# Counting edges by 16 destinations and 8 groups of sources instead of 32 and 4, with the diagonal, the degrees, the folded biases and the loop registers handled otherwise

## The reference

```python
xn = _layernorm(x)
x = x + gnn(xn, edges, L0_gnn_W, L0_gnn_b) + mix(xn, Wq, bq, Wk, bk, Wv, bv, Wo, bo, P)
x = x + ffn(_layernorm(x), Wg, Wu, Wd, Wr, temperature)
# gnn: edges (row, col) = (src, dst), and a self edge (n, n) for every node
h = xn @ W.T + b
deg = zeros(N).at[row].add(1.0)
norm = deg[row] ** -0.5 * deg[col] ** -0.5
out = segment_sum(norm[:, None] * h[col], row, N)
# mix: linear attention, 16 heads of 64; features relu(P . q) and relu(P . k)
# ffn: 8 experts of 128 hidden units, gated silu, routing weights
```

## Time and profile before

| | |
|---|---|
| three runs | 1119.9, 1120.11, 1120.98 us |
| the profiled execution | 1121.14 us, of which the span from first to last instruction is 1119.2 us |
| PE (matmuls) busy | 1098.6 us, 98% of the span, 5707 instructions |
| DVE, ACT, POOL busy | 369.6, 252.9, 287.5 us |
| mean granted TensorE clock | 0.997 |
| counting matmuls | 178 in the fixed parts, 40 in the loops, 40 for self edges |

### The profile page before, as it was taken

One profiled execution on the slowest core, in us unless ns is written; L12 is line 12 of the kernel. 1 busy time (PEld: TensorE's weight loads), 2 busy tenths in 40 slices (PEclk: granted clock), 3 DMA queues, 4 the chain that ended last, 5 costly groups with the idle time before them and its releaser, 6 DMA issues.

```text
span 1119.2 us, 15481 instructions
## 1 busy us (share of the span) xinstructions
PE 1098.6 (98%) x5707; PEld 911.8 (81%) x5707; DVE 369.6 (33%) x991; ACT 252.9 (23%) x398; POOL 287.5 (26%) x232
## 2 busy tenths in 40 slices
PE   5999999999999999999999999999999999999998
PEld 4888778877878888888878888887888888888887
DVE  6854665665623111222212113344321111111111
ACT  4330211112223244311111112334121111112000
POOL 5000011121222146510034443434132223325000
PEclk9999999999999999999999999999999999999999
DMA  6303011222223497704079987775022222216321
GB/s 242 114 29 104 13 29 54 62 61 64 67 91 105 153 306 243 246 1 151 28 193 325 308 242 209 223 225 146 1 86 61 61 61 61 71 52 216 105 102 66
DMA packets 144518, 139.29 MB, mean 124 GB/s; under 512 B 6636, under 2 KB 114492, under 8 KB 144189
## 3 DMA queue, kind: packets, MB, share of 16 engines
q1 hardware_dynamic: 143868, 136.20, 39.0%
q10 hardware_dynamic: 576, 2.10, 0.5%
HBM read 102.32 MB, written 35.96 MB: 124 GB/s over the span
## 4 chain that ended last, share of the span: by engine, by line
PE 97%; DVE 1%; ACT 1%; DMA 1%; issue 0%; POOL 0%; DVEq 0%
PE ps L1549 10%; PE ps L1551 10%; PE ps L1550 10%; PE ps L1817 7%; PE ps L1819 6%; PE ps L1818 6%; PE ps L1759 4%; PE ps L1753 4%; PE ps L1676 3%; PE ps L1677 3%; PE ps L1678 3%; PE ps L1733 3%; PE ps L1865 3%; PE ps L1735 3%; PE ps L1734 3%; PE ps L1864 3%
## 5 line engine op out<-in xcount | busy, mean ns | idle before, releaser
L1549 PE MATMUL ps<-w_hi,xnH 128*128 128x512 f32 x480 | 191.4, 399 | 0.2 <-POOL w_lo L686 0.2
L1550 PE MATMUL ps<-w_lo,xnH 128*128 128x512 f32 x480 | 187.3, 390 | 0.0
L1551 PE MATMUL ps<-w_hi,xnL 128*128 128x512 f32 x480 | 187.2, 390 | 0.0
L1549 PEld LDWEIGHTS ps<-w_hi,xnH 128*128 128x128 f32 x480 | 90.3, 188 | 19.8 <-POOL w_lo L686 0.7
L1551 PEld LDWEIGHTS ps<-w_hi,xnL 128*128 128x128 f32 x480 | 90.2, 188 | 19.4
L1550 PEld LDWEIGHTS ps<-w_lo,xnH 128*128 128x128 f32 x480 | 90.3, 188 | 17.6
L732 POOL TENSOR_TENSOR acc<-acc,cw 128x320 f32<-128x320 f32 x40 | 35.3, 883 | 260.9 <-ACT cw L904 260.0
L1676 PE MATMUL ps<-xnH,w_hi 128*128 128x512 f32 (+1 forms) x192 | 69.2, 360 | 0.0
L1677 PE MATMUL ps<-xnL,w_hi 128*128 128x512 f32 (+1 forms) x192 | 68.3, 356 | 0.0
L1678 PE MATMUL ps<-xnH,w_lo 128*128 128x512 f32 (+1 forms) x192 | 68.0, 354 | 0.0
L1817 PE MATMUL ps<-x2H,guH 128*128 128x512 f32 (+1 forms) x192 | 67.6, 352 | 0.4 <-ACT wT L1084 0.4
(11 more groups left out here) (313 smaller groups left out, 2058.2 us busy)
## 6 DMA issues: line engine op xcount, KB each, us to landing
cR<-c_d SPq DMA_DIRECT2D x20, 640.0 KB, 5.2
foldin<-in SPq DMA_DIRECT2D x32, 256.0 KB, 2.8
guR<-in SPq DMA_DIRECT2D x16, 512.0 KB, 5.3
c_d<-cw SPq DMA_DIRECT2D x40, 160.0 KB
w_raw<-in SPq DMA_DIRECT2D x12, 512.0 KB, 6.5
xb<-in SPq DMA_DIRECT2D x10, 512.0 KB, 4.8
qs0H<-qT_d SPq DMA_DIRECT2D x10, 512.0 KB, 5.4
qs0L<-qT_d SPq DMA_DIRECT2D x10, 512.0 KB, 6.5
```

Source lines behind the costliest of these rows:

```text
L1549: pe.matmul(target, xnH[:, kc, cols], wH[w][:, kc, :], start=(kc == 0), stop=False)
L1550: pe.matmul(target, xnH[:, kc, cols], wL[w][:, kc, :], start=False, stop=False)
L1551: mm = pe.matmul(target, xnL[:, kc, cols], wH[w][:, kc, :], start=False, stop=(kc == KC - 1))
```

## The change

- The first 384 destinations are counted in 24 windows of 16, the others in 28 pairs of windows (32 destinations); sources in 8 groups of 160. A narrow window's matmul has 160 columns and 128 rows (8 groups x 16 destinations). For a pair, `hot1` has 256 places and PE runs two 160-column matmuls per chunk on the same `hot2`. Two narrow windows or one pair share a PSUM bank and are copied, stored and added together, so these are 40 as before.
- `SHARE` sums to 147 instead of 178. With the inputs' sorted destinations, counted out, the loops run 28 times in the 24 narrow windows and 35 times in the 28 pairs. The last fixed chunk of a window stands behind the loop and closes it.
- Self edges: no matmul; POOL adds the identity to each block of C when it is loaded (`own_edges`), and ACT's `count_high` waits for that (`c_own`). The degrees get + 1 from DVE.
- Degrees: two matmuls of 160 columns into 8 x 160, to memory and back as 128 x 10; DVE and ACT use them at j = 5, 6 and 8 instead of 1, 3 and 4.
- Folded biases: one 2-column matmul for both, of each of eight blocks; the result is 128 x 8 and goes to memory in 4-byte pieces.
- Registers: one load of four (two narrow windows) or two (a pair), when a PSUM bank is opened, behind the wait for `win_out`.
- POOL no longer makes `id16`, `idq` and `shifted`; DVE has four more instructions in `edges_keys`.

```diff
-WIN = 32
-NWIN = NP // WIN
-SRCG = NP // 4
-NCHX = NCH + WIN
-SHIFT = SRCG - WIN
+
+WIN = 16
+GROUPS = P // WIN
+SRCG = NP // GROUPS
+NPAIR = NP // (2 * WIN)
+NARROW = 24
+NWIN = NARROW + NPAIR - NARROW // 2
+NCHX = NCH + 32
 RING = 12
-SHARE = [25, 11, 8, 7, 6, 6, 5, 5, 5, 5] + [4] * 7 + [3] * 22 + [1]
+SHARE = [17, 7, 6, 4, 4, 3, 4, 3, 3, 3, 3] + [2] * 13 + [3] * 8 + [2] * 20
...
+def _pair(w):
+
+    return (w // 2, (w % 2,)) if w < NARROW else (w - NARROW // 2, (0, 1))
...
+PAIR_SEEN = [0] + [SEEN[w + 1] for w in range(NWIN) if 1 in _pair(w)[1]]
...
 
-            def store_window(w):
-                t, k = w // 4, w % 4 * WIN
-                sp.wait_ge(win_out, w + 1)
-                sp.dma_start(c_d[t][k:k + WIN, :].rearrange("j (g c) -> g j c", g=4), cw[:, w % 3, :])\
-                  .then_inc(c_st[w % 3], 16)
+            def store_pair(q):
+                t, k = q // 4, q % 4 * 2 * WIN
+                sp.wait_ge(win_out, q + 1)
+                for h in range(2):
+                    rows = c_d[t][k + h * WIN:k + (h + 1) * WIN, :].rearrange("j (g c) -> g j c", g=GROUPS)
+                    sp.dma_start(rows, cw[:, q % 3, h * SRCG:(h + 1) * SRCG]).then_inc(c_st[q % 3], 16)
...
-            sp.dma_start(fb_d[:, :], fbrow[:]).then_inc(fb_st, 16)
+            sp.wait_ge(bias_ev, 2)
+            with nc.allow_non_contiguous_dma(reason="1024 sums"):
+                sp.dma_start(fb_d.rearrange("o (c q) -> q (o c)", q=P), bkf[:]).then_inc(fb_st, 16)
...
+                if j == 2:
+                    sp.wait_ge(dg, 1)
+                    sp.dma_start(deg_d.rearrange("(g c) -> g c", g=GROUPS), drow[:]).then_inc(deg_st, 16)
+                if j == 3:
+                    sp.wait_ge(deg_st, 16)
+                    with nc.allow_non_contiguous_dma(reason="1280 degrees"):
+                        sp.dma_start(dtmp[:, 0, :], deg_d.rearrange("(t q) -> q t", q=P)).then_inc(in_deg, 16)
...
+            def own_edges(i):
+                t, k = i % NT, i // NT * 2 + i % 2
+                pool.wait_ge(in_c[i % 2], 16 * (i // 2 + 1))
+                pool.tensor_tensor(cR[k][:, t, :], cR[k][:, t, :], ident[:], ALU.add).then_inc(c_own, 1)
...
-            def window_out(w):
-                act.wait_ge(win_mm, w + 1)
-                if w >= 3:
-                    act.wait_ge(c_st[w % 3], 16 * (w // 3))
-                    act.wait_ge(acc_step, w - 2)
-                act.activation(cw[:, w % 3, :], bank(6 + w % 2, SRCG), ACT.Copy).then_inc(win_out, 1)
+            def pair_out(q):
+                act.wait_ge(hot_used, PAIR_SEEN[q + 1])
+                if q >= 3:
+                    act.wait_ge(c_st[q % 3], 32 * (q // 3))
+                    act.wait_ge(acc_step, q - 2)
+                act.activation(cw[:, q % 3, :], bank(6 + q % 2, 2 * SRCG), ACT.Copy).then_inc(win_out, 1)
...
-            def hot_pair(target1, target2, w, column, ready):
-                dve.tensor_scalar(target1, iota[:, 0:P], key1[:, column], -512.0 * w, ALU.subtract, ALU.is_equal)
-                dve.tensor_scalar(target2, iota[:], key2[:, column], None, ALU.is_equal).then_inc(ready, 1)
+            def hot_pair(hot_rows, hot_cols, w, column, ready):
+                q, halves = _pair(w)
+                n = len(halves) * P
+                dve.tensor_scalar(hot_rows[:, 0:n], iota[:, 0:n], key1[:, column], -float(2 * P * q + P * halves[0]),
+                                  ALU.subtract, ALU.is_equal)
+                dve.tensor_scalar(hot_cols, iota[:, 0:SRCG], key2[:, column], None, ALU.is_equal).then_inc(ready, 1)
...
-                if end == SEEN[w + 1]:
-                    stop = dve.value_load(rng[0:1, 1, w:w + 1], min_val=2, max_val=NCHX - 1)
-                for n in range(begin, end):
+                closes = end == SEEN[w + 1]
+                if begin == SEEN[w] and 0 in _pair(w)[1]:
+                    k = 2 if w < NARROW else 1
+                    dve.load(span[0:2 * k], rng[0:1, w:w + k, :].rearrange("o w k -> o (w k)"))
+                    for i in range(k):
+                        ranges[w + i] = (dve.snap(span[2 * i], min_val=0, max_val=NCH - 1),
+                                         dve.snap(span[2 * i + 1], min_val=2, max_val=NCHX - 1))
+                first, stop = ranges[w]
+
+                def counted(n):
                     if n >= RING:
                         dve.wait_ge(hot_used, n - RING + 1)
                     hot_pair(hot1[:, n % RING, :], hot2[:, n % RING, :], w, bass.ds(first + (n - SEEN[w]), 1), hot_ready)
-                if end < SEEN[w + 1]:
+
+                for n in range(begin, end - 1 if closes else end):
+                    counted(n)
+                if not closes:
                     return
                 p = w % 2
                 with dve.Fori(first + SHARE[w], stop) as j:
...
+                counted(end - 1)
...
                 if j == 1:
                     dve.wait_ge(deg_mm, 1)
-                    dve.tensor_copy(dtmp[:, 0, :], bank(6, NT)).then_inc(dg, 1)
-                    dve.tensor_reduce(degi[:, 0:1], bank(6, NT), AX_X, ALU.max).then_inc(dg_max, 1)
-                if j == 4:
+                    dve.tensor_scalar(drow[:], bank(6)[0:GROUPS, 0:SRCG], 1.0, None, ALU.add).then_inc(dg, 1)
+                if j == 5:
+                    dve.wait_ge(in_deg, 16)
+                    dve.tensor_reduce(degi[:, 0:1], dtmp[:, 0, :], AX_X, ALU.max).then_inc(dg_max, 1)
+                if j == 8:
...
             def folded_biases():
                 pe.wait_ge(in_const, 48)
                 for c in range(KC):
-                    pe.matmul(bank(6 + c // 4)[0:1, c % 4 * P:(c % 4 + 1) * P], bkc[:, c:c + 1], pbd_s[:, c, :],
-                              start=True, stop=True)
-                for c in range(KC):
-                    mm = pe.matmul(bank(5)[:, c:c + 1], pbd_s[:, c, :], bqc[:, c:c + 1], start=True, stop=True)
+                    mm = pe.matmul(bank(5)[:, 2 * c:2 * c + 2], pbd_s[:, c, :], bkq[:, :, c], start=True, stop=True)
...
             def window(w, begin, end):
-                p, target = w % 2, bank(6 + w % 2, SRCG)
-                if w >= 2:
-                    pe.wait_ge(win_out, w - 1)
-                else:
-                    pe.wait_ge(edge_step, EDGE_STEPS)
-                    pe.wait_ge(consts, CONSTS)
-                for n in range(begin, end):
+                p, (q, halves) = w % 2, _pair(w)
+                if 0 in halves and begin == SEEN[w]:
+                    if q >= 2:
+                        pe.wait_ge(win_out, q - 1)
+                    else:
+                        pe.wait_ge(edge_step, EDGE_STEPS)
+                        pe.wait_ge(consts, CONSTS)
+                    k = 2 if w < NARROW else 1
+                    pe.load(span[0:2 * k], rng[0:1, w:w + k, :].rearrange("o w k -> o (w k)"))
+                    for i in range(k):
+                        ranges[w + i] = (pe.snap(span[2 * i], min_val=0, max_val=NCH - 1),
+                                         pe.snap(span[2 * i + 1], min_val=2, max_val=NCHX - 1))
+                first, stop = ranges[w]
+                closes = end == SEEN[w + 1]
+
+                def count(hot_rows, hot_cols, used, opening=False, closing=False):
+                    for i, h in enumerate(halves):
+                        mm = pe.matmul(bank(6 + q % 2)[:, h * SRCG:(h + 1) * SRCG], hot_rows[:, i * P:(i + 1) * P], hot_cols,
+                                       start=opening and h == 0, stop=closing and h == 1)
+                    mm.then_inc(used, 1)
+
+                for n in range(begin, end - 1 if closes else end):
                     pe.wait_ge(hot_ready, n + 1)
-                    pe.matmul(target, hot1[:, n % RING, :], hot2[:, n % RING, :], start=(n == SEEN[w]), stop=False)\
-                      .then_inc(hot_used, 1)
-                if end < SEEN[w + 1]:
+                    count(hot1[:, n % RING, :], hot2[:, n % RING, :], hot_used, opening=n == SEEN[w])
+                if not closes:
                     return
-                first = pe.value_load(rng[0:1, 0, w:w + 1], min_val=0, max_val=NCH - 1)
-                stop = pe.value_load(rng[0:1, 1, w:w + 1], min_val=2, max_val=NCHX - 1)
                 with pe.Fori(first + SHARE[w], stop):
                     n = pe.snap(rests[p])
                     pe.wait_ge(rest_ready[p], n + 1)
-                    pe.matmul(target, rest1[:, p, :], rest2[:, p, :], start=False, stop=False)\
-                      .then_inc(rest_used[p], 1)
+                    count(rest1[:, p, :], rest2[:, p, :], rest_used[p])
                     pe.reg_add(rests[p], rests[p], 1)
-                g, col = w // 10, SHIFT + w // 10 * WIN - w % 10 * WIN
-                pe.matmul(target, idq[:, g, :], shifted[:, col:col + SRCG], start=False, stop=True)\
-                  .then_inc(win_mm, 1)
+                pe.wait_ge(hot_ready, end)
+                count(hot1[:, (end - 1) % RING, :], hot2[:, (end - 1) % RING, :], hot_used, closing=True)
...
```

(59 more changed lines are left out.)

135 lines of the change are left out of this document (66 added, 69 removed).

## The result

| | before | after |
|---|---|---|
| median | 1120.55 us (1119.9 to 1121.38) | 1144.58 us (1142.89 to 1147.16, 4 runs) |
| span of the profiled execution | 1119.2 us | 1145.4 us |
| mean granted clock | 0.997 | 0.988 |
| all counting portions, each up to the next other matmul | 39.4 us for 258 matmuls | 53.4 us for 309 |

The runs of before are those made beside after, with the first three. The ratio is 1.0219 (95% interval 1.0202 to 1.0236): the change makes the kernel slower by 24 us. The forecast was 1104.5 us, with 0.94 on faster. It was wrong in sign. The profiled execution of after is the slowest of its four, so that the two traces part by 26 us and the medians by 24.

A forecast was written before the change was run, and what follows sets the result against it. PE, busy 98% of the span, was taken to bound the kernel. Terms -13.5 + 4.5 - 1.8 - 1.75 - 3.1 = -15.65 took 1121.1 to 1105.5, and the median 1.0 lower to 1104.5 us; 8 in 10 range 1100 to 1112.

The forecast's parts named there:

- counting matmuls and stalls: PE's counting steps: 309 matmuls at 0.069 us instead of 258 at 0.135, -13.5 us; stalls of PE's queue, +4.5 us.
- folded biases: Stage 0: 16 two-column matmuls instead of 32 instructions, -1.8 us; the result's 4-byte pieces cost 0.
- degrees, and the clock's old falls: Four 160-column instructions for the degrees, -1.75 us; both old falls to about half clock gone, -3.1 us.
- identity in C: POOL's add between C's load and ACT's copy, under 0.5 us; PE comes 1.7 us later, so 0.
- DVE behind it: Counting steps: DVE, busy 130 of 218 us, makes 210 one-hot pairs instead of 218 and has more room: 0.
- the store: Folded-bias result in 1024 4-byte pieces, bounded by a 5.2 us load of 1280 pieces, wanted some 60 us later: 0.
- The third rival: PE waits for SP's small pieces (degree store, 4-byte load, fold inputs in one queue): 1126.5 us, slower than before; chance 0.03.
- the counting matmul: A 160-column f16 counting matmul on PE costs 0.069 us, if the next weights load beside it within 0.067 us.
- the rival of weight loads: Weight loads set the counting matmuls' pace, 0.112 us per 160 columns: 1115.3 us; chance 0.10.
- a third opening: Counting steps closing two banks and opening a third, where PE can't queue: six of 1.3 us, 8 us.
- The rival on the clock: Six stretches with over 1 us of stall in the counting steps call the clock down: 1112.4 us; chance 0.12.

The follow-up runs named there:

- experiment 6: The kernel after with one fixed chunk more in the 11 twice-looping windows and the folded-bias store and reload behind the folds' inputs: 1105.34 us, ratio 0.9874 against before.
- experiment 1: The kernel after with SHARE raised by one in the 11 windows whose loop runs twice, so every loop runs once: 1112.33 us, ratio 0.9939 against before.
- experiment 4: The kernel after with the store and load of the folded bias moved behind the last fold input of stage 0 in SP's queue: 1137.76 us.
- experiment 2: The kernel before with SHARE lowered by one in 11 windows, whose loops then run twice: 1157.64 us, ratio 1.0331 against before.
- experiment 3: The kernel after with second passes kept, but two buffers per parity for the loops' one-hots, used in turn: 1119.99 us, ratio 1.0001 against before.
- experiment 5: The kernel before with only the new folded biases, two-column matmuls and the 4-byte store at its old place: 1125.86 us, ratio 1.0051 against before.
- experiment 7: The kernel after with both faults out, and PE loading a bank's registers ahead of its wait for win_out: 1101.97 us, ratio 0.984 against before.

## Why the prediction was wrong

Against the kernel of experiment 6, whose only differences from after are the two faults, the steps can be held one by one, in the traces:

| step of the prediction | forecast | measured, before to experiment 6 |
|---|---|---|
| counting matmuls and stalls | -13.5 + 4.5 = -9.0 | -8.3 (39.4 to 31.1) |
| folded biases | -1.8 | -2.3 (first counting matmul 102.3 to 100.0) |
| degrees, and the clock's old falls | -1.75 - 3.1 = -4.85 | -4.3 (q products 131.0 to 126.7) |
| products between the counting portions | no term | -0.6 |
| identity in C | 0 | 0 |
| sum | -15.65 | -15.5 (last matmul 1115.51 to 1100.05) |

The medians of the runs made beside each other part by less, 13.9 us (1119.27 to 1105.34, by the interval 12.4 to 15.8): the profiled execution of before, 1121.14 us, lies above its medians. That 1105.34 comes so near to 1104.5 is thus in part luck.

| the two zeros | forecast | measured |
|---|---|---|
| DVE behind it: "It has more room than before: 0" | 0 | +32.3 (experiment 1 against after) |
| the store: "It is wanted some 60 us later: 0" | 0 | +6.8 (experiment 4 against after) |

From the forecast's 1104.5 these two lead to 1143.6; after has 1144.6. In the other order, experiment 4 to 6 and experiment 1 to 6, the two are worth 32.4 and 7.0 us: they add up.

**The step that failed** is *DVE behind it*. It counted DVE's instructions and compared them with its idle time. Busy time came out as said, a little lower (362 us against 370), and was still wrong as an answer, because it did not ask when DVE may begin each of them. The number was at hand: the section on the change has 28 and 35 passes for 24 and 28 windows, 63 for 52, so eleven windows loop twice; before, 40 windows had 40 passes. The prediction priced the extra passes on PE's sequencer and not on the buffer. A second pass makes DVE wait for PE *within* a portion, so DVE's lead over PE, some 5 us in each step, is lost, and PE pays what DVE still has to make, 0.34 us a pair. With the clock that falls behind these waits it is 32.3 us where the prediction has 0. The wait on `rest_used` is in the unchanged code of the loop: the new numbers in `SHARE` make it bind, and no line of the diff touches it.

**The second** is the store in *Folded biases*. The bound was taken from rows 14, 1280 pieces of 512 bytes in 5.2 us, as if pieces were the price, and the question was when the result is wanted, not what stands behind it. 4-byte writes took 11.4 us, over twice that, and what paid was what stood behind them, the loads of x above all: 6.8 us where the prediction has 0. The third rival had the right mechanism, small pieces in SP's queue, but at the degrees and with 0.03: there the pieces are read, in 3.2 us, and nothing waits.

**Right:** the counting matmul. Five in a row have a length of 0.51 us and a single one 0.23, so they start (0.51 - 0.23) / 4 = 0.07 us apart (at 204.29 and 204.22 in experiment 6):

```profile
204.22 0.23 PE L1678 MATMUL ps<-rest,rest 128*128 128x160 f16 x1
204.29 0.51 PE L1678 MATMUL ps<-hot,hot 128*128 128x160 f16 x5
```

Their weight loads still last 98 ns, so f16 loads hide beside 160 columns, and the rival of weight loads falls. The Trainium skill ("TensorE: Matmul & The Clock Gate") fits with its doubled rate for weights of a type other than f32 (Fast Weight Load); its 81 ns between matmuls of 128 columns (the section on the back-to-back gap) is not what this trace shows for 160, and the measurement decides. The size of a third opening was nearly right as well: 1.3 us each at six places were forecast, and in experiment 6 seven portions take 0.8 to 1.4 us longer than their matmuls need, 8.0 together. All stalls are 31.1 - 21.3 = 9.8 us for the forecast's 8. The degrees now take four matmuls:

```profile
360.00 0.71 PE L1750 MATMUL ps<-acc,qmask 128*8 128x160 f32 x4
```

0.6 us to the next start instead of 2.3, and the fold behind them runs at full clock. The identity is 0.46 us on POOL for each block, and PE never waits for it.

**The rival on the clock** (stalls call it down) had the right effect for the wrong stalls. Seven openings of up to 1.3 us between full products bring no fall at all: the clock of experiment 6 is 1.00 throughout. With DVE's lateness, in portions of 2.5 to 4.9 us, it falls six times.

What stays open: in after, experiments 2, 3, 4 and 5 there is one fall some 24 us behind the start of the router's matmuls, behind twenty 8-column matmuls in 2.4 us, while before and experiments 1, 6 and 7 pass the same place at full clock. It costs 1.6 us. The runs don't show what decides it.

## What to carry to other kernels

Between two engines that hand blocks to each other, compare not their busy times but their leads: for every buffer ask how many blocks the producer may be ahead, and count it again for each loop that may now run once more. A constant that only deals out work (here `SHARE`) can thus make an unchanged wait bind. Of a DMA in small pieces ask what stands behind it in the queue, and don't price pieces that are written by a row of pieces that are read (here 11.4 us against 3.2); and load what doesn't depend on a wait ahead of it.

## What the runs showed of the hardware

- 1024 pieces of 4 bytes written to memory took 10.0 to 12.0 us in seven kernels; 1280 pieces of 4 bytes read took 3.0 to 3.2 us in six. A 512 KB load that was issued right behind the writes took 12.7 us, against a median of 6.2.
- f16 matmuls of 160 columns start 0.07 us apart with new weights each time, while a single weight load lasts 0.098.
- Ahead of the six falls to half clock (1.2 GHz) in the counting steps of after, PE was busy for 1.4 to 2.1 of 3.4 us. Five other late portions, of 2.6 to 4.0 us, and seven openings of up to 1.3 us between full steps (experiment 6) brought none.
